# Six single row maxima moved from the expert tiles into the next turn's first score slots, in a two-layer transformer kernel

## The reference, cut to what matters

```
layer 0:  16 heads of 8 channels, softmax(q k / sqrt 8) v, projection
          ffn: inputs, weights and hidden values quantised to 4 bits in blocks of 16,
               silu(gate) * up, then down (128 -> 352 -> 128)
layer 1:  the same attention with biases
          ffn: one shared expert and the best 2 of 8 experts (128 -> 512 -> 128) per token
```

## Time and profile before

| | us |
|---|---|
| median of 3 runs | 1478.62 (1476.63 to 1479.34) |
| the profiled execution | 1480.99 |
| its span | 1479.2 |
| PE busy | 1287.3 (87%) |
| DVE busy | 1074.9 (73%) |
| ACT busy | 788.0 (53%) |
| POOL busy | 401.7 (27%) |

### The profile page before, as it was taken

The page is one execution under the profiler, slowest core; times in us unless marked ns, Lnnn a source line. Parts: engine busy times, 40 slices in busy tenths (PEclk is TensorE's granted clock), DMA queues, the critical chain, the costliest instruction groups (busy, mean ns, idle before and its releaser), DMA issues.

```text
span 1479.2 us, 22025 instructions
## 1 busy us (share of the span) xinstructions
PE 1287.3 (87%) x7829; PEld 609.3 (41%) x7829; DVE 1074.9 (73%) x1907; ACT 788.0 (53%) x1279; POOL 401.7 (27%) x459
## 2 busy tenths in 40 slices
PE   1578789989999889998899899998899988999886
PEld 1113365334633256233553346332563336433641
DVE  8876789677985689766895779856896679824641
ACT  1145235754477534864357544776348643687355
POOL 6001333114231222314231233313223142303331
PEclk8669599999999999999999999999999999999998
DMA  3303373317514364226533275143642264203730
GB/s 111 100 9 109 119 219 106 99 54 219 161 47 127 96 183 144 86 64 190 150 97 104 65 200 168 40 128 96 192 134 92 58 198 144 90 5 104 223 100 15
DMA packets 120734, 171.76 MB, mean 116 GB/s; under 512 B 18153, under 2 KB 98354, under 8 KB 120626
## 3 DMA queue, kind: packets, MB, share of 16 engines
q0 software_dynamic: 27168, 90.44, 20.2%
q1 hardware_dynamic: 92514, 79.38, 18.3%
q10 hardware_dynamic: 944, 0.54, 0.1%
HBM read 116.88 MB, written 52.89 MB: 115 GB/s over the span
## 4 chain that ended last, share of the span: by engine, by line
PE 53%; DVE 28%; ACT 11%; issue 3%; DVEq 3%; DMA 2%; POOL 0%; ACTq 0%; POOLq 0%
DVE nm L913 19%; PE sums L1321 11%; PE mx L1329 11%; ACT ex L702 9%; PE ring L1211 8%; PE mx L1280 4%; PE ring L1410 3%; PE ring L1217 3%; PE sums L1422 3%; PE ring L1206 3%; PE ring L1280 2%; PE sums L1377 2%; PE ring L1259 2%; PE ring L1399 1%; DVE qk_f L851 1%
## 5 line engine op out<-in xcount | busy, mean ns | idle before, releaser
L702 ACT ACTIVATE ex<-mx 128x1024 f32<-128x1024 f32 x512 | 496.0, 1028 | 178.6 <-PE mx L1329 177.2
L913 DVE TENSOR_REDUCE nm<-mx 128x2 f32<-128x1024 f32 x422 | 490.2, 1215 | 68.1 <-PE mx L1280 68.1
L1329 PE MATMUL mx<-qs,ks 128*128 128x512 bf16 (+1 forms) x1024 | 287.6, 391 | 29.4 <-ACT ex L702 14.9
L715 ACT ACTIVATE ex<-ring,wx_sb 128x128 f32<-128x128 f32 x480 | 136.8, 368 | 222.6 <-PE ring L1410 222.6
L1280 PE MATMUL mx<-ks,qs 64*128 64x512 bf16 x844 | 162.6, 406 | 57.2 <-DVE nm L913 55.5
L1329 PEld LDWEIGHTS mx<-qs,ks 128*128 128x128 bf16 (+1 forms) x1024 | 80.2, 99 | 252.5 <-ACT ex L702 170.8
L552 POOL DMA_INDIRECT wx_sb<-wx,wx_row x120 | 114.6, 955 | 255.0 <-PE sums L1422 240.4
L917 DVE TENSOR_REDUCE nm<-ring 128x1 f32<-128x512 f32 x180 | 115.8, 685 | 62.7 <-PE ring L1280 61.6
L1410 PE MATMUL ring<-xsT,wx_sb 128*128 128x128 f32 x960 | 135.9, 285 | 8.5 <-ACT xsT L656 5.4
L1321 PE MATMUL sums<-ex,vs 128*18 128x512 f32 x1024 | 137.6, 610 | 0.0
L1422 PE MATMUL sums<-wx_sb,ex 128*128 128x128 f32 x960 | 135.6, 284 | 0.0
(11 more groups left out here) (191 smaller groups left out, 1403.0 us busy)
## 6 DMA issues: line engine op xcount, KB each, us to landing
scratch<-parts SPq DMA_DIRECT2D x64, 384.0 KB
ks<-scratch SPq DMA_DIRECT2D x256, 64.0 KB, 2.3
qs<-scratch SPq DMA_DIRECT2D x256, 64.0 KB, 2.2
scratch<-parts SPq DMA_DIRECT2D x32, 256.0 KB
xs<-x_sorted POOLq DMA_DIRECT2D x24, 256.0 KB, 7.5
o_sorted<-xs POOLq DMA_DIRECT2D x24, 256.0 KB, 2.8
rest<-parts SPq DMA_DIRECT2D x32, 128.0 KB
x_sb<-x SPq DMA_DIRECT2D x8, 256.0 KB, 3.3
```

What stands on the lines that cost most here:

```text
L702: act.activation(ex[:, ex_buffer(l, b, k), 2 * i:2 * i + 2, :], mx[bank][:, :, :], ACT.Exp, scale=SCALE).then_inc(mx_free[bank], 1)
L715: last = act.activation(ex[:, free_buffer(it, "tiles"), c, i % TG * P:i % TG * P + P], bank[:, c * P:(c + 1) * P], ACT.Silu, bias=wx_sb[n ...
L913: dve.tensor_reduce(nm[l][:, t, h:h + 2], mx[bank][:, :, :], AX.X, ALU.max, negate=True).then_inc(mx_free[bank], 1)
L1329: return pe.matmul(bank, ks[l][r, h, s * P:(s + 1) * P], qs[l][r, h, :], start=True, stop=True)
```

## The change

Of layer 1's 32 pairs of maxima, 29 stay in tiles 3 to 14. The last three pairs (29, 30, 31, all of the last two heads, tiles t = 1 to 3) are made in the next turn as six single tiles through the ring, two each behind the scores of layer 0's slots 1, 2 and 3. PE's transposes of the maxima move from ahead of slot 2 to ahead of slot 4. DVE's order at the turn's start becomes: late maxima 1, `norm_stats`, late maxima 2, `norm_apply`, late maxima 3, the rows' copies, `hidden(0)` to `hidden(3)`. The last sequence keeps its 32 pairs where they were.

```diff
@@
+LATE_PAIRS = 3
+M1_SLOT = LATE_PAIRS + 1
@@ def maxima_of_tile
-    return [(1, pair) for pair in range(NPAIR * (i - steps) // (NTILE - steps), NPAIR * (i + 1 - steps) // (NTILE - steps))]
+    n, left = NTILE - steps, NPAIR - LATE_PAIRS
+    return [(1, pair) for pair in range(left * (i - steps) // n, left * (i + 1 - steps) // n)]
+
+
+def late_pair(k):
+
+    return NPAIR - LATE_PAIRS + k - 1 if 1 <= k <= LATE_PAIRS else None
@@ def ring_uses
-        r = [("m1", it - 1)] if it else []
+        r = [("L", *tile) for k in range(1, LATE_PAIRS + 1) for tile in tiles_of_pair(late_pair(k))] + [("m1", it - 1)] if it else []
@@ vector
+            def late_maxima(part, it, k):
+                for h, t in tiles_of_pair(late_pair(k)):
+                    bank, free = from_ring(part, it, ("L", h, t))
+                    dve.tensor_reduce(nm[1][:, t, h:h + 1], bank[:, :], AX.X, ALU.max, negate=True).then_inc(free, 1)
@@ vector, turn
+                if it > 0:
+                    late_maxima(part, it, 1)
                 if not last:
                     norm_stats(0, it + 1)
-                hidden(0)
-                if it > 0:
-                    max_rows(1, part, it, it - 1)
+                if it > 0:
+                    late_maxima(part, it, 2)
                 if not last:
                     norm_apply(0, it + 1)
+                if it > 0:
+                    late_maxima(part, it, 3)
+                    max_rows(1, part, it, it - 1)
+                hidden(0)
                 hidden(1)
@@ tensor, max_rows
-                turn = it if l == 0 else b
-                for pair in (NPAIR - 2, NPAIR - 1):
-                    pair_read_out(pe, part, turn, ("M", l, pair))
+                if l == 1 and b < it:
+                    for tile in tiles_of_pair(NPAIR - 1):
+                        read_out(pe, part, it, ("L", *tile))
+                else:
+                    for pair in (NPAIR - 2, NPAIR - 1):
+                        pair_read_out(pe, part, it, ("M", l, pair))
@@ tensor, turn
-                    if k == 2 and it > 0:
+                    if k == M1_SLOT and it > 0:
                         max_rows(1, part, it, it - 1)
@@
                     slot_scores(0, part, it, k)
+                    if it > 0 and late_pair(k) is not None:
+                        for tile in tiles_of_pair(late_pair(k)):
+                            late_maxima(part, it, *tile)
                     weighted_sums(0, part, it, it, k - 1)
@@ tensor
+            def late_maxima(part, it, h, t):
+                if (h % 2, t) == (0, 0):
+                    pe.wait_ge(stack_in[1][h // 2], it * N_STACK)
+                bank, full = to_ring(part, it, ("L", h, t))
+                products(1, bank[:, :], h, t).then_inc(full, 1)
```

## The result

| | before | after |
|---|---|---|
| median, us | 1478.98 (1476.63 to 1480.54, 4 runs) | 1509.01 (1503.77 to 1511.01, 4 runs) |
| profiled execution, us | 1480.99 | 1511.01 |
| its span, us | 1479.2 | 1509.3 |
| mean granted clock of PE | 0.948 | 0.934 |

The change makes the kernel slower: the ratio of the times is 1.0197, with a 95% interval of 1.0177 to 1.0218, or +30 us where +12.4 was forecast. The direction was right; 1509.01 us lies above the range of 1481 to 1504.

A forecast was written before the change was run, and what follows sets the result against it. No engine bounds every stage; VectorE narrowly bounds tiles 3 to 14. Six turns at 4.3 - 2.5 = +1.8 us and a last turn at +1.6 gave +12.4 on the 1478.62 median: 1491.0 us, range 1481 to 1504.

The forecast's parts named there:

- DVE's idle time ahead of the maxima: Turn start: DVE waits for PE's scores until +4.9 us after slot 0's first score pair, 4.0 us idle.
- Last bank and rows: Layer 0's early slots: last bank read at +11.1, PE waits 0.8 us, DVE copies rows at +11.9, 0.65 us later.
- h_sb and split at +31.7: Layer 0's slots: h_sb done and q/k split started at +31.7, split 7.1 us later; PE waits 0.3 us more.
- Stack whole at +50.4, PE's wait 2.5: Layer 1's slot 1: first head pair's stack lands 18.7 us after the split; PE waits 2.5 us, 4.3 us later overall.
- Rivals 1 and 2: DVE's idle time swallows the delay, 1466 us, chance 0.08; or no stack wait comes, 1476.0 us, chance 0.08.
- Tiles 2.5: Expert tiles 3 to 14: 29 pairs instead of 32 save 2.5 us per turn, seven times.
- nothing later in the turn pays it back: Behind PE's stack wait in layer 1: the 4.3 us delay stays, because PE leads from there on.
- rival 3: Behind the new 2.5 us PE wait the clock halves for 3.4 us, up to 1.7 us a turn: 1501 us, chance 0.15.
- The last turn: No split or x statistics: h_sb ready at +31.1 where PE asked at +27.0, 4.1 us later.

The follow-up runs named there:

- the profile from the second chip: Changed kernel run and traced again, beside the kernel before on that chip: 1506.06 us, ratio 1.0188.
- the order alone: Kernel before with only the change's order of DVE work and PE transposes, no maximum moved: 1.017 on the first chip; 1506.94 us, 1.0208 on the third.

## Why the prediction was right and wrong

- **DVE's idle time ahead of the maxima**: 4.0 forecast, 3.94 measured. Last bank and rows: the copies were forecast at +11.9 and came at +11.98, behind 0.80 us of idle time where the forecast had 0.8.
- **h_sb and split at +31.7**: measured +32.0 and +31.9. PE waited 0.60 for h_sb in slot 12, where 0.3 was forecast.
- **Stack whole at +50.4, PE's wait 2.5**: product at +51.0, wait 2.62 with a DMA as releaser. Rivals 1 and 2 fall here. The delay of that product was 4.85 us in the mean against 4.3, which makes 3.3 us over six turns. The chain from split to first reload took 465.81 - 450.81 = 15.0 us, and the product started 4.1 behind that; I had 16.5 + 2.3 to the landing of the fourth, with 0.1 off for a good case, where the product starts 19.1 behind the split.
- **Tiles 2.5**: 2.3 measured, 2.2 in the mean; the forecast was 2.4 us too favourable in all. Turn 0's share is not certain: the kernel before itself starts turn 1 at 242.33 on the second chip and at 245.56 in the first profile, a larger difference than the 1.8 us put down to the change.
- **The step that failed is the one on the clock.** The forecast's sum has the line "nothing later in the turn pays it back" and takes everything behind the wait as unchanged. It put the clock at nothing there; the clock stood outside the sum as rival 3, priced at 1.7 us a turn and given 0.15. In the profiled execution the fall came in all six turns and cost 1.2 to 2.7 us each, 9.5 in all, the largest of the terms that make the missing 17.7 us. The price was about right (10 us for six turns; 7.4 in the profile from the second chip) and the chance was too small; what misled me was that the trace of before showed a fall only behind 3.4 us of idling. The runs add a limit: the fall is not certain in each turn (four of six on the second chip, four of six with the order alone), and how often it comes in the runs that were not traced is not known. The term alone does not make the miss: with it the forecast would be 1501 us, and 3.3 us from a longer chain, 3.2 from the last turn and 2.4 from the tiles and turn 0 come on top.
- **The last turn**: 4.1 forecast, 7.3 measured. h_sb came at +34.1 in the turn that started at the lower clock, and the clock fell once more at PE's wait of 3.70 us for it. On the second chip, without that start, h_sb came at +31.75; PE waited 3.57 us, the clock fell there too, and the last turn took 156.08 us, where the kernel before took 150.14 on that chip. So of the 3.2 us missed here some 2.4 go with the turn's start at the lower clock, and not with the forecast chain.
- **What was never in the sum**: turns that start at the lower clock (turn 5 and the last in the first profile, turn 4 on the second chip). Each delays h_sb by some 2 us.

The mechanism up to the wait was forecast rightly and not by luck: the idle time, the split, the wait and its releaser all lie within 0.6 us of their forecasts. I had also written that the idle time costs more than the six reductions do. The runs bear that out: with the same reductions in another order the cost is gone, and the order without them costs 2.1%.

**Open**: why the same wait in the same program is followed by the lower clock in one execution and not in another; why some turns start at the lower clock and others don't; how much of the 30 us is the clock's in the median of the runs; and what slowed the first chip behind the ranks.

## What to carry to other kernels

An operation moved to another place on an engine that works in order costs, beside its own time, all the idle time that it puts in front of the work due there; follow that work through every engine and queue to its next deadline, and put what is ready in front of what has to wait (here the same six maxima gave +1.9% in one order and -0.3% in the other). A late result can also be mended at its deadline: using the stack one slot later took back two thirds. Where a change brings a new wait of some 2 to 4 us in front of TensorE, put the clock that it may lose behind it into the sum, and not only into the range.

## What the runs showed of the hardware that I had not expected

- TensorE's granted clock fell to 0.50 at waits of 1.67, 1.71, 2.62, 2.75, 3.13 and 3.70 us, and stayed at 1.00 at others of 1.70, 1.73, 2.06, 2.62 and 3.09 (the last in turn 4 of the order experiment on the first chip), in part in the same turn of the same program. The fall lasted 3.4 or 6.8 us and cost 1.2 to 2.7 us from the first maximum to the ranks. Within this range the length of the wait did not tell which it would be.
- It also fell where no long wait stood: at turn starts, behind 3.4 us with PE busy for 2.10. In one traced execution that came in every turn from the second on (turns of 174 us), in others in none to three of the turns.
- One chip of three took about 2% longer with every kernel tried on it, nearly all of it in one stretch of the turn, from the ranks to the shared expert.
